# One more dt*u*B pair on POOL and one more C pair on DVE in the last batch of a Mamba and low-rank expert kernel

## The chip, the cores and the metric

The kernel runs on one core of a Trainium2 chip. The metric is the device time of one execution in microseconds, the median of several runs. All arithmetic is in float32.

## The reference, cut to what matters

Four batches of 512 rows of 512 channels pass through two residual blocks. The first one is a selective state-space scan (16 states for each of 512 channels) over a context input, and its output is gated by silu of the normalised `x`. The second is a top-2 choice of 32 low-rank experts on the normalised result. The part that the change touches is the scan:

```python
def step(state, xs):
    d_t, B_t, C_t, u_t = xs
    dA = jnp.exp(d_t[..., None] * A)
    state = state * dA + (d_t * u_t)[..., None] * B_t[:, None, :]
    y_t = jnp.einsum('ben,bn->be', state, C_t)
    return (state, y_t)
...
y = y + D[None, :, None] * u
y = y * jax.nn.silu(z)
```

The expert block then computes `sc = h @ Wr.T`, the two best of 32, `hU`, its gated product with `V`, and adds it to the residual.

## The kernel before, in words

Channels lie on the 128 partitions and time on the free axis, so that one instruction of DVE scans one state of 128 channels over a whole row of time. The work is cut into **phases** `f`. A phase is one batch, one block of 128 channels (`k` from 0 to 3) and a stretch of time: 512 steps in batches 0 to 2 (phases 0 to 11), 256 steps in the last batch, which is gone through in two halves (phases 12 to 15 with `c0` = 0, phases 16 to 19 with `c0` = 256). Where the first half ends, the last column of each state is kept in `carry`, and the second half starts from it. `SPLIT` is 12 and `LAST` is 19.

A phase has 16 **tiles** `n`, one for each state, or 8 **pairs** `p` of two. For each tile the program makes
- the decay exp(delta * A), by ACT (`decay`, L1016),
- the product dt*u*B, in one of two ways: by PE, as matmuls of the transposed `du` with diagonal matrices of B, into a PSUM bank (`make_dbu`, L759), or by POOL for a pair at a time into SBUF (`times_b`, L571). `POOL_SETS[b]` lists the pairs by POOL for each batch,
- the scan, by DVE (`scan`, L1267). For a tile by PE, the product lies in one of the three banks `p_s` and the decay in the ring `da`; for a tile by POOL it is the decay that lies in the bank. Either way a tile holds bank `g % 3`, with g = 16f + n, and the bank is free again when its scan (or its product with C out of the bank) is done (`wait_for_bank`),
- the product with C: by POOL for a pair in SBUF (`times_c`, L586), or by DVE for the pairs in `PAIRS_BY_DVE`, whose scans are written to the bank and read out of it (`times_c` of DVE, L1285),
- the sum over states: PE transposes each tile into `p_y` (`add_y`, L781).

Every engine's order is written out by hand in program order; an engine never passes a waiting instruction. Between the tiles of phase f lie the steps of the expert block of earlier tiles of rows: `best_two` (DVE, after the scan of tile 2), `gates` (DVE, after the scans of tiles 4 to 6; the last result is `gw`, L1364), `copy_gated` (ACT, L972, placed after the decay of tile 5), the product with V (PE, `times_v`, L814, at tiles 5 to 7), the product with U (PE, `times_u_weights`, L805, from tile 8 on; it waits for `gw`), and `gate_y` (DVE, L1293 and L1301, after the scans of tiles 8 and 9), for which PE's `skip` (L770) of the next phase's sum waits.

The diagonal matrices of B are written into `pair_b` at the start of a batch by POOL (`diagonals`, L544), by ACT for the last PE pair; for POOL's pairs the rows of B are broadcast into the same place by SP's queue (`broadcast_b`, L419), as those of C are into `c_bc`. `dbu` has room for two pairs: `times_b` waits for the scans of the pair before the last one (`ve_scan`). POOL also makes `du` of the next phase (`times_u`, L556) and small scales (`scale_of_f`, L605 and L607; in phases 13 and 14 these stand right after the first dbu of the next phase).

In the last batch before the change, POOL makes dbu of pairs 0, 2, 3, 5, 6, PE those of pairs 1, 4, 7. DVE multiplies pairs 1 and 4 with C (in phase 19 pair 7 as well), POOL the others. POOL takes the first two dbu of the coming phase after its C pairs 5 and 6 of the current one:

```python
times_c(f, 5)
if next_first:
    times_b(f + 1, pool_pairs(PHASE[f + 1][0])[0])
...
times_c(f, 6)
if next_first and len(pool_pairs(PHASE[f + 1][0])) == 5:
    times_b(f + 1, pool_pairs(PHASE[f + 1][0])[1])
...
times_c(f, 7)
```

Of the kernel before, what the change touches and what calls it, by code (L numbers as in the profile page):

```python
# [22 lines left out]

POOL_SETS = [[2, 5], [1, 3, 5, 7], [1, 3, 5, 7], [0, 2, 3, 5, 6]]


def flamingo(nc, x, ctx_t, g_xattn, g_ffn, in_w_t, conv_w, conv_b, x_w_t, dt_w_t, dt_b, a_log, d_skip,
# [18 lines left out]
    PHASE = [(b, k, 0, L) for b in range(B - 1) for k in range(Q)]  # L46
    PHASE += [(B - 1, k, c0, H) for c0 in (0, H) for k in range(Q)]
    F = len(PHASE)
    LAST = F - 1
    SPLIT = Q * (B - 1)  # L50
# [10 lines left out]
    def pool_pairs(b):  # L61
        return POOL_SETS[b]

    def pe_pairs(b):
        return [p for p in range(PAIRS) if p not in POOL_SETS[b]]

    def by_act(b, p):


        return p == pe_pairs(b)[-1] or b == 0 and p in (0, 6)  # L70
# [26 lines left out]

    PAIRS_BY_DVE = [(LAST, 7)]
    PAIRS_BY_DVE += [(f, p) for f in range(SPLIT, F) for p in (1, 4)]
    PAIRS_BY_DVE += [(f, 1) for f in range(Q - 1, SPLIT)] + [(f, 5) for f in range(Q - 1, SPLIT, Q)]  # L100
# [52 lines left out]
    with ExitStack() as ctx:  # L153
# [362 lines left out]
        def _(eng):  # L516
# [13 lines left out]

            def diagonals(b, i):
                p = pe_pairs(b)[i]
                if by_act(b, p):
                    return
                if i == 0 or b == 0:
# [78 lines left out]
            for f in range(F):  # L614
                b, k, c0, w = PHASE[f]
# [3 lines left out]
                many = len(pairs) >= Q  # L619
                five = len(pairs) == 5  # L620
                next_first = f < LAST and (PHASE[f + 1][0] != b or many)
                times_c(f, 0)
                if five:
                    times_b(f, pairs[2])
                elif many or len(pairs) == 3:
                    times_b(f, pairs[1])
# [5 lines left out]
                times_c(f, 1)  # L632
                if many and not five:
                    times_b(f, pairs[2])
                if turned:
                    diagonals(b, len(pe_pairs(b)) - 1)
                times_c(f, 2)
                if five or not many:
                    times_b(f, pairs[3] if five else pairs[-1])
                early_u = k == 0 and c0 == 0  # L640
# [3 lines left out]
                if many:  # L644
                    times_b(f, pairs[-1])
                if f < LAST and not (early_u and not many):
# [16 lines left out]
                times_c(f, 6)  # L663
                if next_first and len(pool_pairs(PHASE[f + 1][0])) == 5:
                    times_b(f + 1, pool_pairs(PHASE[f + 1][0])[1])
# [850 lines left out]
```

## Time and profile before

| what | value |
|---|---|
| median of three runs | 534.21 us (533.29, 534.21, 534.3) |
| the profiled execution | 533.53 us |
| its span, first to last instruction | 531.8 us |
| granted TensorE clock, mean | 0.978 |
| busy share PE, DVE, POOL, ACT | 92%, 87%, 85%, 71% |
| chain that ended last, by engine | PE 48%, POOL 19%, DVE 13%, ACT 10%, issue 9% |

The profile is of one execution. A row of a timeline gives the start and the duration of an instruction (or of several in a row, with xN) and, in brackets, how long the engine had been idle before it and what released it. Times are microseconds from the start of the span. The last batch (phases 12 to 19) takes from about 366 to 507. The chain goes back from the last instruction through whatever released each step. Instructions that follow each other on one engine overlap by up to a tenth of a microsecond, so that starts, not ends, give the pace.

### The profile page before, as it was taken

The numbers are of one execution on the slowest core, as the hardware profiler recorded it, in microseconds if no ns is written. First come the engines' busy times: TensorE is split into PE (matmuls) and PEld (weight loads), VectorE is DVE, ScalarE is ACT, GpSimd is POOL, SyncE is SP. The second block draws the span as 40 slices with busy tenths as digits, with TensorE's granted clock in tenths as the row PEclk, the third lists the DMA queues.
The fourth block names the chain that finished last, engine by engine and source line by source line (L and its number), as shares of the span: only waits on it lengthen the run. The fifth ranks groups of instructions, "written<-read, shape, count | busy, mean of one in ns | idle before, by whom it ended". The sixth has DMA issues, their size and how long they took to land.

```text
span 531.8 us, 9178 instructions
## 1 busy us (share of the span) xinstructions
PE 491.4 (92%) x3018; PEld 368.0 (69%) x3018; DVE 462.9 (87%) x846; ACT 380.1 (71%) x699; POOL 451.9 (85%) x327
## 2 busy tenths in 40 slices
PE   9989899998787999999999999999899999899688
PEld 5568788687676676668676777767566766676654
DVE  3799799799799999799999999798988989999852
ACT  4698848775876777866958776957868869768542
POOL 1389999959999999989999999889799898888910
PEclk9969799999999999999999999999999999999899
DMA  5595000126520001065230000077100000000001
GB/s 127 176 375 217 0 2 1 41 85 213 182 80 1 1 1 60 1 229 202 71 101 2 20 1 22 8 281 227 45 21 1 22 20 17 6 21 21 2 20 39
DMA packets 18704, 39.36 MB, mean 74 GB/s; under 512 B 5585, under 2 KB 6353, under 8 KB 18658
## 3 DMA queue, kind: packets, MB, share of 16 engines
q1 hardware_dynamic: 18658, 38.79, 21.4%
q8 instruction: 24, 0.39, 0.3%
q14 instruction: 22, 0.18, 0.1%
HBM read 34.33 MB, written 4.46 MB: 73 GB/s over the span
## 4 chain that ended last, share of the span: by engine, by line
PE 48%; POOL 19%; DVE 13%; ACT 10%; issue 9%; DMA 1%; DVEq 0%; SPq 0%; POOLq 0%; ACTq 0%
PE p_s L759 12%; PE p_y L781 11%; POOL state L586 9%; POOL dbu L571 7%; DVE state L1267 6%; PE p_v L814 5%; PE p_f L805 5%; PE p_tr L728 3%; PE p_v L691 2%; ACT da L1016 2%; DVE x L1216 2%; PE p_pr L703 2%; ACT pair_b L1000 1%; PE p_f L794 1%; PE p_pr L682 1%
## 5 line engine op out<-in xcount | busy, mean ns | idle before, releaser
L586 POOL TENSOR_TENSOR state<-state,c_bc 128x1024 f32<-128x1024 f32 (+1 forms) x131 | 256.7, 1970 | 21.6 <-DVE state L1267 19.2
L759 PEld LDWEIGHTS p_s<-pair_b,du_t 128*128 128x128 f32 x1072 | 140.7, 200 | 44.9 <-issue 33.4
L759 PE MATMUL p_s<-pair_b,du_t 128*128 128x128 f32 x1072 | 154.6, 287 | 16.0 <-DVE state L1267 15.8
L781 PE MATMUL p_y<-ident,state 128*128 128x128 f32 x1024 | 149.3, 276 | 0.0
L1016 ACT ACTIVATE p_s<-delta,a_neg 128x512 f32<-128x512 f32 (+1 forms) x162 | 93.7, 583 | 77.6 <-DVE state L1267 44.1
L1267 DVE TENSOR_TENSOR_SCAN state<-da,p_s 128x512 f32<-128x512 f32 (+1 forms) x116 | 134.5, 1172 | 16.0 <-PE p_s L759 13.1
L571 POOL TENSOR_TENSOR dbu<-du,pair_b 128x1024 f32<-128x1024 f32 (+1 forms) x80 | 145.3, 1819 | 0.2 <-DMA pair_b<-bc_rows 0.2
L781 PEld LDWEIGHTS p_y<-ident,state 128*128 128x128 f32 x1024 | 121.5, 144 | 23.3 <-issue 20.2
L1016 ACT ACTIVATE da<-delta,a_neg 128x512 f32<-128x512 f32 (+1 forms) x158 | 99.3, 647 | 18.5 <-DVE state L1267 18.4
L1267 DVE TENSOR_TENSOR_SCAN state<-p_s,dbu 128x512 f32<-128x512 f32 (+1 forms) x100 | 97.6, 996 | 7.6 <-POOL dbu L571 6.0
L805 PE MATMUL p_f<-u_sb,h_t 128*128 128x512 f32 x112 | 55.4, 597 | 2.4 <-DVE gw L1364 2.4
L814 PE MATMUL p_v<-v_sb,hug_t 128*128 128x512 f32 x112 | 55.4, 598 | 0.0
L1285 DVE TENSOR_TENSOR state<-p_s,c_bc 128x256 f32<-128x256 f32 (+1 forms) x58 | 30.5, 526 | 0.7
L544 POOL TENSOR_SCALAR_AFFINE_SELECT pair_b<-b_t 128x1024 f32<-128x1024 f32 x11 | 12.4, 1133 | 19.9 <-ACT b_t L972 19.9
L1267 DVE TENSOR_TENSOR_SCAN state<-p_s,carry,dbu 128x256 f32<-128x256 f32 x40 | 28.0, 734 | 0.8 <-POOL dbu L571 0.7
L805 PEld LDWEIGHTS p_f<-u_sb,h_t 128*128 128x128 f32 x112 | 18.5, 191 | 12.7 <-issue 9.6
L1267 DVE TENSOR_TENSOR_SCAN p_s<-p_s,dbu 128x512 f32<-128x512 f32 x22 | 26.8, 1217 | 0.0
L1216 DVE SCALAR_TENSOR_TENSOR u<-p_pr,cw,u 128x511 f32<-128x511 f32 (+2 forms) x33 | 24.1, 730 | 2.2 <-ACT u L936 2.1
L770 PEld LDWEIGHTS p_y<-ident,skipped 128*128 128x128 f32 x64 | 7.2, 143 | 24.5 <-issue 24.5
L814 PEld LDWEIGHTS p_v<-v_sb,hug_t 128*128 128x128 f32 x112 | 18.1, 190 | 8.4 <-issue 8.3
L556 POOL TENSOR_TENSOR du<-delta,u 128x512 f32<-128x512 f32 (+1 forms) x19 | 19.8, 1043 | 2.8 <-POOL dbu L571 2.8
L682 PE MATMUL p_pr<-cx,w_in 128*128 128x512 f32 x44 | 21.5, 612 | 0.0
(175 smaller groups left out, 640.6 us busy)
## 6 DMA issues: line engine op xcount, KB each, us to landing
c_bc<-bc_rows SPq DMA_DIRECT2D x32, 512.0 KB, 5.1
pair_b<-bc_rows SPq DMA_DIRECT2D x16, 512.0 KB, 5.5
xs<-in_x SPq DMA_DIRECT2D x16, 256.0 KB, 4.6
out<-ot SPq DMA_DIRECT2D x14, 256.0 KB, 2.0
cx<-in_ctx_t SPq DMA_DIRECT2D x4, 512.0 KB, 3.8
u_sb<-in_u_w SPq DMA_DIRECT2D x1, 1024.0 KB, 14.1
v_sb<-in_v_w SPq DMA_DIRECT2D x1, 1024.0 KB, 15.6
w_in<-in_in_w_t SPq DMA_DIRECT2D x1, 384.0 KB, 4.7
```

Source lines behind the costliest of these rows:

```text
L556: eng.tensor_tensor(du[:, 0:w], delta[:, f % 2, 0:w], u[:, (Q * b + k) % U_RING, c0:c0 + w], ALU.mult).then_inc(po_du, 1)
L571: eng.tensor_tensor(dbu[:, i % 2, :, 0:w], du[:, 0:w].unsqueeze(1).to_broadcast([P, 2, w]), rows_of_b(p)[:, :, c0:c0 + w], ALU.mult).then_ ...
L586: eng.tensor_tensor(pair, pair, c_bc[:, 2 * p:2 * p + 2, c0:c0 + w], ALU.mult).then_inc(po_cs, 1)
L682: mm = eng.matmul(conv_bank(q)[:, :], w_in[:, k, e * P:(e + 1) * P], cx[:, k, :], start=(k == 0), stop=(k == KD - 1))
L759: mm = eng.matmul(p_s[g % BANKS][:, t * P:(t + 1) * P], du_t[:, f % 2, t, :], diagonals_of(n // 2)[:, n % 2, c0 // P + t, :], start=(t == ...
L781: mm = eng.matmul(p_y[:, t, :], slot(NS * f + n)[:, t * P:(t + 1) * P], ident[:, :], is_transpose=True, start=False, stop=(n == NS - 1 and ...
L805: mm = eng.matmul(hu_bank(T)[:, :], ht_of(T)[:, k, :], u_sb[:, k, :], start=(k == 0), stop=(k == Q - 1))
L814: mm = eng.matmul(v_bank(T)[:, :], hugt_of(T)[:, k, :], v_sb[:, k, :], start=False, stop=(k == Q - 1), skip_group_check=True)
L1016: eng.activation(to, delta[:, f % 2, 0:w], ACT.Exp, scale=a_neg[:, k, n:n + 1]).then_inc(ac_da, 1)
L1216: eng.scalar_tensor_tensor(out=conv_v(q)[:, s:], in0=conv_bank(q)[:, 0:L - s], scalar=cw[:, q % Q, TAPS - 1 - s:TAPS - s], in1=conv_v(q)[: ...
L1267: eng.tensor_tensor_scan(scanned, decayed, added, first, ALU.mult, ALU.add).then_inc(ve_scan, 1)
L1285: eng.tensor_tensor(slot(g)[:, 0:w], scanned, c_bc[:, n, c0:c0 + w], ALU.mult).then_inc(ve_cs, 1)
```

## The change

In the last batch pair 1 goes from PE to POOL (dbu), and pair 7 from POOL to DVE (C) in all eight phases; the order of POOL's steps is rewritten for six pairs. Diagonals of pair 1 are no longer made, and the rows of B of pair 1 are broadcast in their place. A pair that DVE multiplies with C and POOL gives dbu for now exists in the last batch: both the decay and the scan's result of pair 1 lie in the bank.

```diff
-POOL_SETS = [[2, 5], [1, 3, 5, 7], [1, 3, 5, 7], [0, 2, 3, 5, 6]]
+POOL_SETS = [[2, 5], [1, 3, 5, 7], [1, 3, 5, 7], [0, 1, 2, 3, 5, 6]]
...
-    PAIRS_BY_DVE = [(LAST, 7)]
-    PAIRS_BY_DVE += [(f, p) for f in range(SPLIT, F) for p in (1, 4)]
+    PAIRS_BY_DVE = [(f, p) for f in range(SPLIT, F) for p in (1, 4, 7)]
...
             def diagonals(b, i):
+                if i >= len(pe_pairs(b)) or by_act(b, pe_pairs(b)[i]):
+                    return
                 p = pe_pairs(b)[i]
-                if by_act(b, p):
-                    return
...
-                five = len(pairs) == 5
+                six = len(pairs) == 6
...
                 times_c(f, 0)
-                if five:
+                if six:
                     times_b(f, pairs[2])
...
                 times_c(f, 1)
-                if many and not five:
-                    times_b(f, pairs[2])
+                if many:
+                    times_b(f, pairs[3 if six else 2])
...
                 times_c(f, 2)
-                if five or not many:
-                    times_b(f, pairs[3] if five else pairs[-1])
+                if not many:
+                    times_b(f, pairs[-1])
...
                 times_c(f, 3)
                 if many:
-                    times_b(f, pairs[-1])
+                    times_b(f, pairs[4 if six else -1])
+                if six:
+                    times_b(f, pairs[5])
...
                 times_c(f, 6)
-                if next_first and len(pool_pairs(PHASE[f + 1][0])) == 5:
+                if next_first and len(pool_pairs(PHASE[f + 1][0])) == 6:
                     times_b(f + 1, pool_pairs(PHASE[f + 1][0])[1])
```

POOL's order where phase 14 goes over into phase 15. `dbu` is a pair's dt*u*B, `state<-state,c_bc` a pair's product with C, `carry` the kept column, `fr` the small scale. Before, the first row is dbu of pair 0 of phase 15:

```order
L571 TENSOR_TENSOR dbu<-du,pair_b 128x2x256
L605 TENSOR_TENSOR fr<-fmv,minus_half 128x1
L607 TENSOR_SCALAR fr<-fmv,fr 128x1
L584 COPY carry<-state 128x2
L586 TENSOR_TENSOR state<-state,c_bc 128x2x256
L571 TENSOR_TENSOR dbu<-du,pair_b 128x2x256
L584 COPY carry<-state 128x2
L586 TENSOR_TENSOR state<-state,c_bc 128x2x256
L584 COPY carry<-state 128x2
L586 TENSOR_TENSOR state<-state,c_bc 128x2x256
L571 TENSOR_TENSOR dbu<-du,pair_b 128x2x256
```

The same place in the changed kernel, again from dbu of pair 0 of phase 15 on (its line numbers are one lower on POOL):

```order
L570 TENSOR_TENSOR dbu<-du,pair_b 128x2x256
L604 TENSOR_TENSOR fr<-fmv,minus_half 128x1
L606 TENSOR_SCALAR fr<-fmv,fr 128x1
L583 COPY carry<-state 128x2
L585 TENSOR_TENSOR state<-state,c_bc 128x2x256
L570 TENSOR_TENSOR dbu<-du,pair_b 128x2x256
L583 COPY carry<-state 128x2
L585 TENSOR_TENSOR state<-state,c_bc 128x2x256
L570 TENSOR_TENSOR dbu<-du,pair_b 128x2x256 x2
```

The second dbu stands at the same place in both, but it was that of pair 2 and is now that of pair 1; the product with C of pair 7 has left the queue, and two dbu (pairs 2 and 3) now follow each other.

DVE's order from the end of phase 17 into phase 18, before; the rows after `hug` are tiles 14 and 15 (pair 7), tiles 0 and 1, and tile 2 (the first of pair 1):

```order
L1373 TENSOR_TENSOR hug<-p_f,gw 128x512
L1267 SCALAR_TENSOR_TENSOR state<-da,carry,p_s 128x256 x2
L1267 SCALAR_TENSOR_TENSOR state<-p_s,carry,dbu 128x256 x2
L1267 SCALAR_TENSOR_TENSOR p_s<-da,carry,p_s 128x256
L1323 MAX top<-p_f 128x8
```

And in the changed kernel (line numbers one higher on DVE):

```order
L1374 TENSOR_TENSOR hug<-p_f,gw 128x512
L1268 SCALAR_TENSOR_TENSOR p_s<-da,carry,p_s 128x256
L1286 TENSOR_TENSOR state<-p_s,c_bc 128x256
L1268 SCALAR_TENSOR_TENSOR p_s<-da,carry,p_s 128x256
L1286 TENSOR_TENSOR state<-p_s,c_bc 128x256
L1268 SCALAR_TENSOR_TENSOR state<-p_s,carry,dbu 128x256 x2
L1268 SCALAR_TENSOR_TENSOR p_s<-p_s,carry,dbu 128x256
L1324 MAX top<-p_f 128x8
```

Two products with C have come in between the scans of pair 7, and the scan of tile 2 takes POOL's `dbu` in the place of PE's bank.

## Rows read from the trace of the kernel before

**Rows 1.** Stages: phase 15 (columns: us, busy per engine, PEclk, DMA share, GB/s)

```profile
416.26:434.22 17.96, 17.12 (x99) 11.75 (x98) 15.82 (x47) 12.09 (x30) 16.09 (x20) 1.00 0.08 29
```

**Rows 2.** Chain that ended last, phases 14 and 15 (start us, us, what)

```profile
418.10 0.19 POOL carry L584
...
427.41 1.24 POOL dbu L571
...
432.10 0.46 PE p_s L759 x4
```

**Rows 3.** Timeline of POOL: second dbu for phases 13, 15 and 16

```profile
386.88 1.27 POOL L571 TENSOR_TENSOR dbu<-du,pair_b 128x512 f32<-128x512 f32 x1
...
423.19 1.27 POOL L571 TENSOR_TENSOR dbu<-du,pair_b 128x512 f32<-128x512 f32 x1
...
439.44 1.27 POOL L571 TENSOR_TENSOR dbu<-du,pair_b 128x512 f32<-128x512 f32 x1
```

**Rows 4.** Timeline of DVE: scan of tile 2, phases 13, 15, 16, 17, 18

```profile
386.68 0.67 DVE L1267 TENSOR_TENSOR_SCAN p_s<-da,p_s 128x256 f32<-128x256 f32 x1
...
422.10 0.67 DVE L1267 TENSOR_TENSOR_SCAN p_s<-da,p_s 128x256 f32<-128x256 f32 x1
...
439.61 0.75 DVE L1267 TENSOR_TENSOR_SCAN p_s<-da,carry,p_s 128x256 f32<-128x256 f32 x1
...
458.51 0.73 DVE L1267 TENSOR_TENSOR_SCAN p_s<-da,carry,p_s 128x256 f32<-128x256 f32 x1
...
475.41 0.73 DVE L1267 TENSOR_TENSOR_SCAN p_s<-da,carry,p_s 128x256 f32<-128x256 f32 x1
```

**Rows 5.** Timeline of DVE: phase 15, then phase 17

```profile
423.13 0.20 DVE L1323 MAX8 top<-p_f 128x8 f32<-128x32 f32 x1 [0.36 <-PE p_f L794]
...
428.68 0.69 DVE L1267 TENSOR_TENSOR_SCAN state<-p_s,dbu 128x256 f32<-128x256 f32 x1 [0.97 <-POOL dbu L571]
...
432.59 0.69 DVE L1267 TENSOR_TENSOR_SCAN p_s<-da,p_s 128x256 f32<-128x256 f32 x1 [0.30 <-PE p_s L759]
...
460.22 0.74 DVE L1267 TENSOR_TENSOR_SCAN p_s<-da,carry,p_s 128x256 f32<-128x256 f32 x1
...
461.34 0.74 DVE L1267 TENSOR_TENSOR_SCAN state<-p_s,carry,dbu 128x256 f32<-128x256 f32 x1
...
468.30 0.76 DVE L1267 TENSOR_TENSOR_SCAN p_s<-da,carry,p_s 128x256 f32<-128x256 f32 x1 [0.63 <-PE p_s L759]
...
469.62 2.67 DVE L1267 TENSOR_TENSOR_SCAN state<-p_s,carry,dbu 128x256 f32<-128x256 f32 x4
```

**Rows 6.** Timeline of ACT: phase 15

```profile
424.58 0.58 ACT L972 ACTIVATE hug_t<-p_tr 128x512 f32<-128x512 f32 x1
```

**Rows 7.** Timeline of PE: phase 15, then phase 17

```profile
425.32 1.94 PE L814 MATMUL p_v<-v_sb,hug_t 128*128 128x512 f32 x4
...
429.26 0.61 PE L759 MATMUL p_s<-pair_b,du_t 128*128 128x128 f32 x4
...
465.93 1.88 PE L805 MATMUL p_f<-u_sb,h_t 128*128 128x512 f32 x4
```

**Rows 8.** Timeline of POOL: from phase 11 into phase 12

```profile
363.58 1.09 POOL L544 TENSOR_SCALAR_AFFINE_SELECT pair_b<-b_t 128x1024 f32<-128x1024 f32 x1
...
366.96 1.27 POOL L571 TENSOR_TENSOR dbu<-du,pair_b 128x512 f32<-128x512 f32 x1
368.18 2.37 POOL L586 TENSOR_TENSOR state<-state,c_bc 128x1024 f32<-128x1024 f32 x1
```

**Rows 9.** Timeline of DVE: phase 12, tile 4

```profile
370.05 0.68 DVE L1267 TENSOR_TENSOR_SCAN state<-p_s,dbu 128x256 f32<-128x256 f32 x1
```

**Rows 10.** DMA issues (KB each, median us to landing)

```profile
pair_b<-bc_rows SPq DMA_DIRECT2D x16, 512.0 KB, 5.5
```

**Rows 11.** Stages: two stretches of phase 19, columns as in rows 1

```profile
496.00:500.00 4.00, 1.39 (x8) 1.04 (x8) 3.29 (x7) 2.03 (x5) 4.00 (x4) 0.98 0.01 2
500.00:504.00 4.00, 3.49 (x20) 3.52 (x21) 3.28 (x7) 1.79 (x4) 3.49 (x4) 0.60 0.02 4
```

## The prediction

> **What bounds the kernel now.** I read the stages first. In phase 15 [rows 1], of 17.96 us PE is busy for 17.12 (first figure), DVE for 15.82 (third), POOL for 16.09 (fifth): three engines near their limit, so that a phase's length is set by how they wait for each other, and no share of busy time gives a price. Next the chain that ended last [rows 2]. In phases 14 and 15 it leaves DVE at 418.10, at the end of the scan of tile 11, runs through POOL without a gap, C pair 5, dbu 0, the small scale, C 6, dbu 2, C 7, C 0, dbu 3, and comes back to DVE at the scan of tile 6, which had waited 0.97 us for that last dbu at 428.68 [rows 5]. So **POOL's run after tile 11** is part of the cycle. In it I look for the end of the second dbu [rows 3] beside the start of DVE's tile 2 [rows 4]. Last come the waits of DVE further on in a phase: at tile 2's `MAX8` for PE's scores (0.36), at tile 9 for PE (0.30 in phase 15, 0.63 in phase 17) [rows 5].
>
> **The change part by part.** A tile by PE costs PE 0.46 us [rows 2] (the row of 432.10). Sixteen tiles (pair 1, eight phases) are removed: 7.4 us of PE's work. On POOL a dbu comes and a C pair goes, both 1.27 us [rows 3, 8]; in phase 19, where DVE had pair 7 before, only the dbu comes, but POOL's order up to its third dbu there loses nothing and gains nothing before tile 6. DVE gets the product with C of pair 7. What such a product costs it behind a scan shows in phase 17: from the scan of tile 3 at 460.22 to the next at 461.34 is 1.12 us, against 2.67 / 4 = 0.67 for scans without one [rows 5]. That is 0.45 a tile, 0.9 a pair (I take 1.05 where the last column is kept too, an estimate from the same rows and one more small instruction).
>
> *The new wait.* Tile 2 took its product from PE, early. Now it takes POOL's second dbu, which stands where pair 2's stood, behind C 5, dbu 0, the scale and C 6. Pair 2 was wanted only at tile 4; pair 1 is wanted at tile 2. The second dbu ended at 386.88 + 1.27 = 388.15, 424.46 and 440.71 in phases 13, 15 and 16 [rows 3], and DVE began tile 2 at 386.68, 422.10 and 439.61 [rows 4]: it will be **late by 1.47, 2.36 and 1.10 us**. Phase 14 repeats phase 15. POOL's run up to there starts from tile 11's scan as before and holds nothing that has gone, so none of it gets shorter. DVE's own delay by pair 7 (1.05) lies inside this wait. In phases 17 and 18 POOL has no columns to keep and phase 18 no scale; there the dbu comes with or before DVE, and what counts is DVE's own 0.9.
>
> *What is given back.* Behind tile 2 the wait for scores (0.36) goes, since PE is early; so does the 0.97 at tile 6, since dbu 3 now follows dbu 2 at once and C 7 is out of the queue. But the steps behind tile 2 form a second path: its product with C frees the bank for ACT's decay of tile 5, behind it ACT copies `hug_t` (start 424.58 [rows 6]), PE starts the product with V on it at 425.32, reaches its tile 8 at 429.26 [rows 7], needs 0.46 for that, and from the product with U to tile 9's scan go 468.30 - 465.93 = 2.37 us [rows 5, 7]. From tile 2 to tile 9 that is (424.58 - 422.10 - 0.36) + 0.74 + 3.94 + 0.46 + 2.37 = 9.6 us. Before, it was 432.59 - 422.10 = 10.5. **Given back: 0.9** in phases 14 and 15. In phase 17 it was 468.30 - 458.51 = 9.8, of which the same path leaves 9.5: 0.3, and I use that for 16 and 18. Phase 13 lies between these two; I take 0.5. PE's freed 0.46 a tile lies ahead of the product with V and turns into a wait there: it is worth nothing in this sum.
>
> *Phases 12 and 19.* POOL loses one writing of diagonals (1.09) and gets to the second dbu at 366.96 - 1.09 = 365.87. Behind it come C 7 of phase 11 (2.37) and C 0, and only then dbu 2 [rows 8]: 367.1 + 2.3 + 1.5 + 1.25 = 372.2 (1.5 is C 0 of 256 columns with its kept column, an estimate from 1.27 and the 0.19 of [rows 2]), where DVE wanted tile 4 at 370.05 [rows 9]. Most of this 2.1 falls into waits that are there now for PE and ACT; I take +0.3, between -0.5 (PE's relief counts) and +1.5. In phase 19 nothing of the expert block follows and POOL's third dbu decides as before; +0.2, between -0.5 and +0.9, from pair 7 of phase 18.
>
> *Moved transfers.* SP's queue gets one broadcast more, 512 KB, 5.5 us from issue to landing [rows 10], for pair 1, and its slot goes ahead of that of pair 2. Pair 1 was POOL's in batch 2, so its place is free early in phase 11, long before use. The broadcasts of C behind it wait for POOL's own reading of the old rows, not for the queue. Cost nothing; without that cover a landing would come later by up to one broadcast, 5.5 us. In pair 1 ACT's decay now goes into the bank and so waits for the scan or the product three tiles before; DVE stands waiting at tile 2 in that time, which hides it; otherwise it costs up to one decay, about 0.5. A scan with both operands in other memory (`dbu` and bank in place of `da` and bank) has no such row at 256 columns. The nearest scans are 0.67 to 0.69 for either kind [rows 4, 5]; bounds -0.05 and +0.1 a tile, 0 taken.
>
> *Sum.* 12: +0.3. 13: 1.47 - 0.5 = +1.0. 14 and 15: 2.36 - 0.86 = +1.5 each. 16: 1.10 - 0.3 = +0.8. 17 and 18: 0.92 - 0.3 = +0.6 each. 19: +0.2. Together **+6.4 us**. The profiled execution took 533.53, so the same one would take 539.9; the median of the runs is 0.7 above it, and my forecast for the median is 540.6. Ends of this case, from the bounds above: +3 (give-backs of 1.4 a phase) to +8.
>
> **TensorE's clock.** The row first: in phase 19 PE is busy for 1.39 of 4 us, and in the next 4 the granted clock is 0.60, that is 1.2 GHz for most of them [rows 11]; that cost (1 - 0.60) x 4 = 1.6 us of its time. In the changed phases 13 to 15 PE stands idle for about 3 of 5 us ahead of the product with V: 1.3 of removed work, plus the 2.4 by which tile 2 is late, less what PE was behind. The Trainium skill ("TensorE: Matmul & The Clock Gate", on HAM oscillation) warns of just this, that waits between bursts throttle the array and each burst then starts at half clock; by it the sum would rise in all three phases. The sum above has no such fall; it is a rival.
>
> **The rivals.**
> - *The clock falls in one to three phases.* For: the row of phase 19. Against: the pause here is shorter and broken by a microsecond and a half of matmuls. PE's path is then the critical one, so each fall counts in full: 540.6 + 1.6 = 542.2, or 545.4 for three.
> - *PE set the pace, and it gets faster.* For: 95% busy in rows 1, and DVE waits for PE at tile 9. If the second dbu were there when DVE comes to tile 2, at most 1.05 us later than now, the phases would be shorter by PE's 0.92 each: 534.2 - 7.4 = 526.8. It decides whether POOL's run from tile 11 to the second dbu (424.46 - 418.10 = 6.4 us) is shorter than DVE's way there (4.0 + 1.05). It is not, by 1.3 us; POOL would have to run ahead, which its wait on tile 11 forbids. Where the two are level, in 17 and 18, half of the gain is possible.
> - *No change.* The lateness of tile 2 is caught up whole before tile 9, because the copy of `hug_t` can go sooner than I think, and pair 7 is hidden: 534.2 to 537.
> - *The change does not do what it says*: the order rows show that it does; no chance.
>
> **How the numbers follow.** The forecast case (537.2 to 542) has a chance of 0.58; the clock 0.24; faster 0.09; little change 0.09. About 0.2%, 1.1 us, can be told from no change by a measurement of this kernel. Faster by more than that: 0.09. Within it, half of the fourth case: 0.05. Slower: 0.86. The range takes in the forecast case whole, the upper half of the last one and two and a half falls of the clock: 535.0 to 545.0.
>
> **What would show each step.** In the changed profile: DVE's scan of tile 2 waits for POOL's dbu, about 1.3 us in phases 14 and 15, less in 13 and 16, near zero in 17 and 18; no wait for POOL at tile 6 in 13 to 18; PE idle ahead of the product with V in 13 to 15; DVE's products of pair 7 add 14 instructions; phase 15 takes 19.4 us instead of 17.96. POOL's busy time stays within 2 us. I am wrong if tile 2 does not wait, if tile 9 follows tile 2 by less than 9 us, or if PE's clock falls outside phase 19.

## The result and the profile after

| | before | changed |
|---|---|---|
| median | 534.25 us (4 runs, 533.29 to 535.01) | 551.84 us (4 runs, 549.47 to 554.63) |
| profiled execution, its span | 533.53, 531.8 us | 549.47, 547.7 us |
| granted TensorE clock, mean | 0.978 | 0.963 |

The ratio is 1.0335, 95% interval 1.0306 to 1.0364: 17.6 us slower. The direction was forecast; the size was not. 540.6 was expected, and the range ended at 545.0. The runs of the changed kernel also lie 5.2 us apart, three times as far as those of before.

The page of the changed kernel (busy tenths and granted clock in 40 slices of 13.7 us):

```profile
PE 492.4 (90%) x2954; PEld 362.8 (66%) x2954; DVE 469.9 (86%) x868; ACT 381.0 (70%) x699; POOL 451.9 (83%) x323
...
PE   8969898989687999999989999999779899899588
...
PEclk9979899999899999999999999999999799699799
...
PE 46%; POOL 18%; DVE 14%; ACT 12%; issue 9%; DMA 1%; DVEq 0%; SPq 0%; ACTq 0%; POOLq 0%
```

Busy shares fall by one or two points and the chain has nearly the shares of before. What stands out is the line `PEclk`. Before, it reads 9 from the slice of 67 us up to the last batch's end, where a single 8 stands. Now the last batch (366 to 523 us) has a 7 in the slice of 424 us, a 6 in that of 465 and a 7 in that of 506. So I cut the last batch at the same event in both traces, the start of DVE's scan of tile 11, and looked at the stretches that end in phases 14, 15 and 17. Before (columns as in [rows 1]):

```profile
399.38:417.34 17.96, 17.12 (x98) 11.76 (x97) 15.81 (x47) 15.65 (x34) 16.23 (x21) 1.00 0.05 16
417.34:434.52 17.18, 16.34 (x93) 11.21 (x92) 15.07 (x46) 11.37 (x28) 15.67 (x20) 1.00 0.04 16
452.35:470.29 17.94, 16.04 (x93) 11.04 (x92) 16.70 (x45) 11.49 (x28) 15.87 (x16) 1.00 0.04 16
```

The same three in the changed kernel, and below them the pieces of each in which the granted clock is at half:

```profile
400.42:421.39 20.97, 17.82 (x90) 11.26 (x89) 16.96 (x51) 15.72 (x34) 16.01 (x19) 0.92 0.04 13
421.39:443.02 21.63, 18.57 (x85) 11.37 (x84) 16.21 (x50) 11.61 (x28) 16.02 (x19) 0.84 0.04 13
461.57:484.82 23.25, 19.80 (x85) 13.00 (x84) 17.52 (x47) 11.80 (x28) 15.97 (x16) 0.78 0.03 12
410.17:413.60 3.43, 3.28 (x4) 1.41 (x5) 3.15 (x14) 3.28 (x12) 2.61 (x4) 0.51 0.00 0
430.50:437.50 7.00, 6.20 (x11) 2.91 (x12) 5.10 (x19) 4.38 (x13) 5.10 (x7) 0.51 0.00 0
468.10:478.40 10.30, 9.97 (x29) 6.58 (x30) 7.68 (x25) 6.82 (x18) 6.98 (x8) 0.50 0.00 1
```

PE executes eight records fewer in each stretch and is busy longer, 18.57 us against 16.34 in phase 15, because for 7.0 us it runs at 1.2 GHz in place of 2.4 (a granted clock of 0.51). POOL's work is unchanged within 0.4 us. Over the span, the stretches of phases 14, 15 and 17 grow by 3.01, 4.45 and 5.31 us, 12.8 of the 15.9 by which the span grows.

What PE did before it fell is in its timeline (changed kernel, phases 14, 15 and 16, then 17):

```profile
410.32 3.55 PE L815 MATMUL p_v<-v_sb,hug_t 128*128 128x512 f32 x4 [1.67 <-ACT hug_t L973]
...
426.25 0.41 PE L729 MATMUL p_tr<-ident,zh 128*128 128x128 f32 x2 [0.98 <-ACT h_t L973]
...
431.31 3.75 PE L815 MATMUL p_v<-v_sb,hug_t 128*128 128x512 f32 x4 [1.68 <-ACT hug_t L973]
...
451.96 1.95 PE L815 MATMUL p_v<-v_sb,hug_t 128*128 128x512 f32 x4 [0.54 <-ACT hug_t L973]
...
468.43 0.66 PE L729 MATMUL p_tr<-ident,zh 128*128 128x128 f32 x2 [2.52 <-ACT h_t L973]
```

In 14 and 15 PE waits twice, about 1.0 us for ACT's copy of `h_t` and 1.7 us for that of `hug_t`; the clock falls in the second wait, and the product with V, 1.94 us in [rows 7], takes 3.55 and 3.75. In 16 the wait is 0.54 us, the clock holds and the product takes 1.95. In 17 the wait of 2.52 us comes earlier, and the clock stays at half through 9.97 us of busy matmuls out of 10.3. What that does to DVE is seen in its timeline (changed kernel: tile 2 and tile 9 of phase 15, then `MAX8` and tile 9 of phase 17):

```profile
428.54 0.70 DVE L1268 TENSOR_TENSOR_SCAN p_s<-p_s,dbu 128x256 f32<-128x256 f32 x1 [1.22 <-ACT p_s L1017]
...
438.92 0.70 DVE L1268 TENSOR_TENSOR_SCAN p_s<-da,p_s 128x256 f32<-128x256 f32 x1 [2.97 <-PE p_s L760]
...
470.67 0.20 DVE L1324 MAX8 top<-p_f 128x8 f32<-128x32 f32 x1 [1.47 <-PE p_f L795]
...
480.67 0.76 DVE L1268 TENSOR_TENSOR_SCAN p_s<-da,carry,p_s 128x256 f32<-128x256 f32 x1 [3.05 <-PE p_s L760]
```

Tile 2 waits as forecast. Tile 9, which waited 0.30 and 0.63 us for PE in [rows 5], now waits 3 us.

### The profile page after: what moved, and what is told of

It reads as the page before. It is cut to its first block, busy times and chain, and to the rows that moved or that the text cites. A ratio compares the mean times of both kernels' runs of the same rounds, so it can differ in the third digit from the quotient of the medians.

```text
span 547.7 us, 9076 instructions
## 1 busy us (share of the span) xinstructions
PE 492.4 (90%) x2954; PEld 362.8 (66%) x2954; DVE 469.9 (86%) x868; ACT 381.0 (70%) x699; POOL 451.9 (83%) x323
## 4 chain that ended last, share of the span: by engine, by line
PE 46%; POOL 18%; DVE 14%; ACT 12%; issue 9%; DMA 1%; DVEq 0%; SPq 0%; ACTq 0%; POOLq 0%
PE p_s L760 10%; PE p_y L782 10%; POOL state L585 8%; PE p_v L815 7%; POOL dbu L570 6%; DVE state L1268 6%; PE p_f L806 5%; PE p_tr L729 3%; ACT da L1017 2%; PE p_v L692 2%; ACT p_s L1017 2%; DVE x L1217 2%; ACT pair_b L1001 2%; DVE p_s L1268 1%; PE p_pr L704 1%
## 5 line engine op out<-in xcount | busy, mean ns | idle before, releaser
L585 POOL TENSOR_TENSOR state<-state,c_bc 128x1024 f32<-128x1024 f32 (+1 forms) x124 | 247.8, 2009 | 28.5 <-DVE state L1268 26.5
L1017 ACT ACTIVATE p_s<-delta,a_neg 128x256 f32<-128x256 f32 (+1 forms) x178 | 101.2, 573 | 89.8 <-DVE state L1286 45.2
L760 PEld LDWEIGHTS p_s<-pair_b,du_t 128*128 128x128 f32 x1008 | 130.0, 197 | 41.1 <-issue 31.1
L570 POOL TENSOR_TENSOR dbu<-du,pair_b 128x512 f32<-128x512 f32 (+1 forms) x88 | 154.5, 1766 | 0.6 <-DMA pair_b<-bc_rows 0.3
L760 PE MATMUL p_s<-pair_b,du_t 128*128 128x128 f32 x1008 | 141.2, 283 | 13.6 <-DVE state L1268 13.3
L1268 DVE TENSOR_TENSOR_SCAN state<-da,p_s 128x512 f32<-128x512 f32 x108 | 129.3, 1209 | 14.7 <-PE p_s L760 11.9
L1017 ACT ACTIVATE da<-delta,a_neg 128x512 f32<-128x512 f32 (+1 forms) x142 | 91.8, 663 | 18.3 <-DVE state L1268 18.3
L815 PE MATMUL p_v<-v_sb,hug_t 128*128 128x512 f32 x112 | 62.0, 661 | 4.7 <-ACT hug_t L973 4.5
L1286 DVE TENSOR_TENSOR state<-p_s,c_bc 128x256 f32<-128x256 f32 (+1 forms) x72 | 36.4, 506 | 0.9
L1268 DVE TENSOR_TENSOR_SCAN p_s<-p_s,dbu 128x512 f32<-128x512 f32 (+1 forms) x30 | 32.3, 1077 | 3.5 <-ACT p_s L1017 2.4
L815 PEld LDWEIGHTS p_v<-v_sb,hug_t 128*128 128x128 f32 x112 | 20.2, 211 | 15.9 <-issue 15.8
L806 PEld LDWEIGHTS p_f<-u_sb,h_t 128*128 128x128 f32 x112 | 18.5, 191 | 12.8 <-issue 9.6
```

The lines of the kernel that those rows point to most:

```text
L570: eng.tensor_tensor(dbu[:, i % 2, :, 0:w], du[:, 0:w].unsqueeze(1).to_broadcast([P, 2, w]), rows_of_b(p)[:, :, c0:c0 + w], ALU.mult).then_ ...
L585: eng.tensor_tensor(pair, pair, c_bc[:, 2 * p:2 * p + 2, c0:c0 + w], ALU.mult).then_inc(po_cs, 1)
L760: mm = eng.matmul(p_s[g % BANKS][:, t * P:(t + 1) * P], du_t[:, f % 2, t, :], diagonals_of(n // 2)[:, n % 2, c0 // P + t, :], start=(t == ...
L806: mm = eng.matmul(hu_bank(T)[:, :], ht_of(T)[:, k, :], u_sb[:, k, :], start=(k == 0), stop=(k == Q - 1))
L815: mm = eng.matmul(v_bank(T)[:, :], hugt_of(T)[:, k, :], v_sb[:, k, :], start=False, stop=(k == Q - 1), skip_group_check=True)
L1017: eng.activation(to, delta[:, f % 2, 0:w], ACT.Exp, scale=a_neg[:, k, n:n + 1]).then_inc(ac_da, 1)
```

## The experiments

Times are compared with runs of the kernel before on the same chip. Two questions stood open: how much of the 17.6 us is the clock's, and what the rest is made of. A matmul of the identity with itself into the block of `p_y` that is unused in these phases (`fill`) keeps PE busy and delays nothing as long as it lies in a wait.

**1. The changed kernel with PE's waits filled** (`fill`). The table's first number stands ahead of `turn_sz` at tile 2, the second ahead of `times_v` at tile 5. By the table these are 46 matmuls, 92 records in the trace (the expectation says 42).

```diff
+            def fill(count):
+                for i in range(count):
+                    eng.matmul(p_y[:, 3, :], ident[:, :], ident[:, :], start=False, stop=False,
+                               skip_group_check=True)
+
+            FILL = {13: (9, 1), 14: (4, 6), 15: (4, 6), 16: (1, 2), 17: (9, 1), 18: (1, 2)}
...
+                        fill(FILL.get(f, (0, 0))[0])
                         if f:
                             turn_sz(f - 1)
...
                     if n == 5 and tail >= 0:
+                        fill(FILL.get(f, (0, 0))[1])
```

> The changed kernel, with matmuls of the identity into an unused block of p_y where PE waits in phases 13 to 18 (ahead of the turn of silu(z) and of the product with V; 3 to 10 a phase, 42 in all, about 9 us of PE). Theory A: the clock stays at 2.4 GHz in phases 13 to 18, and the 6 windows of half clock there, 1.6 us each, go: 541 to 544 us, the late dbu stays. If the clock is not what stretches phases 14, 15 and 17: 551 us or more, since PE only got more work.

Measured: 541.81 us (541.49 to 542.04), ratio 1.0145 [1.0122, 1.0167]. The same three stretches of this kernel:

```profile
400.89:419.47 18.58, 17.67 (x105) 12.44 (x104) 16.14 (x49) 14.91 (x32) 15.42 (x19) 1.00 0.01 2
419.47:438.83 19.36, 18.56 (x110) 13.00 (x109) 16.91 (x51) 12.26 (x30) 16.01 (x20) 1.00 0.07 28
457.00:476.00 19.00, 17.56 (x103) 12.24 (x102) 17.48 (x47) 11.69 (x29) 15.31 (x16) 1.00 0.06 22
```

(The first is 0.8 us short of a whole stretch, and the second begins with that piece; phase 14 takes 19.39 us from tile 11 to tile 11 and phase 15 takes 18.58.) More work on PE, and the kernel is 10.0 us faster: with more to do PE keeps a granted clock of 1.00. In phase 15 its timeline reads

```profile
423.99 1.06 PE L835 MATMUL p_y<-ident 128*128 128x128 f32 x8
...
428.36 1.50 PE L835 MATMUL p_y<-ident 128*128 128x128 f32 x12
430.17 1.96 PE L815 MATMUL p_v<-v_sb,hug_t 128*128 128x512 f32 x4 [0.31 <-ACT hug_t L981]
```

The product with V starts 1.65 us behind the matmul that stands ahead of the fillers, as in the changed kernel (1.68), but it takes 1.96 us. The runs lie 0.55 us apart, where those of the changed kernel lie 5.2 apart. So the spread goes with the falls: over the changed kernel's four runs the mean clock goes from 0.963 in the fastest to 0.951 in the slowest.

**2. The removed matmuls put back as idle ones** (`same_pe`): four identity matmuls in each of phases 13 to 18, where tiles 2 and 3 were made.

```diff
+            FILL = {f: (4, 0) for f in range(13, 19)}
```

> The changed kernel, with four matmuls of the identity in phases 13 to 18 at the place of the removed tiles 2 and 3, so that PE has the same work as before and the engines' other work is as changed. If the removed work itself opens the way to the half clock, the falls go and it takes 541 to 544 us. If it is the waiting time behind it (the product with V waits for the copy of hug_t, 1.7 us in phases 14 and 15), it stays at 547 to 552 us.

Measured: 547.24 us (ratio 1.0259 [1.0232, 1.0286]), but the five runs are 541.96 and then 546.93, 547.24, 547.28 and 547.86. The run of 541.96 is the profiled one, and it has no fall in phases 13 to 18:

```profile
400.80:419.50 18.70, 16.43 (x92) 10.92 (x91) 16.21 (x50) 14.96 (x33) 15.52 (x19) 1.00 0.00 1
419.50:438.90 19.40, 17.23 (x96) 11.62 (x97) 16.91 (x51) 12.62 (x31) 16.07 (x20) 1.00 0.08 28
457.00:476.00 19.00, 16.63 (x95) 11.20 (x92) 17.48 (x46) 12.15 (x29) 15.19 (x17) 1.00 0.08 29
```

Of the other four only the mean clock is on record, 0.956 to 0.963 against 0.972. So the same program takes 542 us where the clock holds and 547 us where it is lower; with the removed work put back as four fillers a phase it can come out either way.

**3. `h_t` copied one tile sooner** (`h_first`). A tuning idea against the waits for `h_t`.

```diff
-                    if n == (1 if mid % Q else 2) and mid >= 0:
+                    if n == ((1 if mid % Q else 2) if f < SPLIT else (0 if mid % Q else 1)) and mid >= 0:
                         copy_h(mid)
```

> The changed kernel, with ACT's copy of h_t one tile sooner in the last batch (ahead of the decay of tile 1, in phases 13 and 17 ahead of the decay of tile 2), so that it no longer stands behind a decay that waits for DVE's product of pair 7. Theory D (the decays in the bank hold up h_t, PE waits 2.6 us for it in phases 13 and 17 and 1.0 in 14 and 15, and this idle time brings the clock down): 543 to 548 us, no fall in phases 13 and 17. Theory A alone (only the dbu at tile 2 matters): 549 to 553 us.

Measured: 550.13 us (548.07 to 551.81), 1.0312 [1.0271, 1.0354]. From the waits of phases 12 to 19, first of the changed kernel, then of this one (us in total, times, longest):

```profile
PE p_tr L729 <- ACT h_t L973: 7.9, 6, 2.6
```

```profile
PE p_tr L729 <- ACT h_t L973: 3.6, 6, 1.5
PE p_tr L729 <- ACT sz_t L973: 5.1, 6, 2.3
```

The wait halved, 2.3 us of the 4.3 came back as one for the next copy, `sz_t` (2.8 us in 3 waits in the changed kernel), and the clock still falls, from 386.4 to 393.2, 410.3 to 417.2, 434.2 to 437.7 and 468.4 to 478.6. Idle time that moves is still idle.

**4. One half of the change alone.** C of pair 7 to DVE in all phases, nothing else (`c7_alone`, against before):

```diff
-    PAIRS_BY_DVE = [(LAST, 7)]
-    PAIRS_BY_DVE += [(f, p) for f in range(SPLIT, F) for p in (1, 4)]
+    PAIRS_BY_DVE = [(f, p) for f in range(SPLIT, F) for p in (1, 4, 7)]
```

> The kernel before, with the product of pair 7 with C on DVE in all eight phases of the last batch and nothing else changed. Theory A (the late second dbu of POOL makes tile 2 wait, PE then idles and its clock falls): pair 1 still comes from PE, so tile 2 does not wait and the clock falls in phase 19 alone; DVE has 14 products more, of which POOL's shorter run to the third dbu gives back about 1 us in phases 14 and 15. 534 to 539 us. Theory B (the products of pair 7 on DVE are what costs): 545 us or more, as the changed kernel.

Measured: 543.15 us (539.65 to 544.39), 1.0157 [1.011, 1.0204]. And dbu of pair 1 to POOL alone, the reverse edit on the changed kernel (`dbu1_alone`):

```diff
-    PAIRS_BY_DVE = [(f, p) for f in range(SPLIT, F) for p in (1, 4, 7)]
+    PAIRS_BY_DVE = [(LAST, 7)]
+    PAIRS_BY_DVE += [(f, p) for f in range(SPLIT, F) for p in (1, 4)]
```

> The changed kernel, with the product of pair 7 with C back on POOL (phase 19 excepted, as before). Theory A: the second dbu ends at the same distance from tile 11, DVE gets to tile 2 about 1 us sooner and waits that much longer, and POOL's queue is a product longer up to the third dbu: 548 to 556 us, with the clock at 1.2 GHz in several phases. Theory B: under 538 us.

Measured: 551.35 us (549.27 to 554.42), 1.031 [1.0276, 1.0345]. Both halves bring falls of the clock in phases 13 to 18: `c7_alone` one of 10.2 us in phase 13, `dbu1_alone` four, in 13, 14, 15 and 17. The first shows a way that I had not seen at all. Its PE timeline in phase 13, and the stretch behind:

```profile
386.33 0.93 PE L758 MATMUL p_s<-pair_b,du_t 128*128 128x128 f32 x4 [1.73 <-DVE state L1284]
```

```profile
386.70:396.90 10.20, 10.20 (x35) 7.51 (x35) 7.44 (x28) 5.93 (x16) 6.91 (x9) 0.50 0.01 2
```

Tile 2's matmuls need the bank of tile 15 of the phase before, which DVE's product of pair 7 now holds. PE waits 1.73 us for it, and then it is busy for 10.20 of 10.20 us at half clock.

**5. Both halves with the clock held** (`c7_fill`: `c7_alone` with 28 identity matmuls ahead of tile 2; `dbu1_fill`: `dbu1_alone` with the table of experiment 1).

```diff
+            FILL = {13: 7, 14: 5, 15: 5, 16: 2, 17: 7, 18: 2}
...
+                    if n == 2:
+                        fill(FILL.get(f, 0))
                     if (f, n) in by_pe:
                         make_dbu(f, n)
```

> The kernel c7_alone with 28 matmuls of the identity in phases 13 to 18, ahead of PE's tile 2, where PE waits 1.2 to 1.7 us a phase for DVE's product of tile 15 to free the bank. c7_alone took 543.2 and had three windows at half clock in its profile. With the clock held, about 1.6 us a window go: 538 to 540 us, which is the price of the product of pair 7 beside a PE tile 2. If the filler comes on top of PE's path: 543 us or more.

> The kernel fill with the product of pair 7 with C back on POOL. Theory A: in phases 13 to 16 DVE's work for pair 7 lies in the wait at tile 2 and costs nothing, while C 7 in POOL's queue puts off dbu 2 and 3 by 1.5 us: 542 to 545 us. Rival E: the products of pair 7 are what costs: 536 to 539 us.

Measured: `c7_fill` 539.97 us (538.73 to 540.4), 1.0105 [1.0084, 1.0126]; `dbu1_fill` 546.12 us (545.02 to 546.35), 1.0227 [1.0208, 1.0245]. Neither has a fall in phases 13 to 18. By the ratios, and in this kernel's 534: pair 7 on DVE costs 5.6 us, dbu of pair 1 on POOL costs 12.1, both together 7.7 (experiment 1). With pair 7 on POOL the third dbu, tile 4's, has one more C product ahead of it; DVE in phase 15 of `dbu1_fill`, tiles 2 and 4:

```profile
427.57 0.70 DVE L1277 TENSOR_TENSOR_SCAN p_s<-p_s,dbu 128x256 f32<-128x256 f32 x1 [2.30 <-POOL dbu L571]
...
431.75 0.69 DVE L1277 TENSOR_TENSOR_SCAN state<-p_s,dbu 128x256 f32<-128x256 f32 x1 [1.52 <-POOL dbu L571]
```

So moving pair 7 is right given the first move (it gives 4.4 us back), and wrong without it. In all three kernels the clock falls later on, from about 505 us, for 6.8, 10.2 and 6.8 us, and these prices hold what that costs. From tile 11 of phase 11 to tile 11 of phase 19 alone, the three are 4.9, 11.4 and 7.8 us longer than before, in the same order.

**6. Is tile 2's wait the whole of what remains?** First both dbu of the coming phase ahead of C 5 (`early_dbu`), then the same with the fillers of experiment 1 (`early_fill`):

```diff
+                front = next_first and f >= SPLIT
+                if front:
+                    times_b(f + 1, pool_pairs(PHASE[f + 1][0])[0])
+                    times_b(f + 1, pool_pairs(PHASE[f + 1][0])[1])
                 times_c(f, 5)
-                if next_first:
+                if next_first and not front:
...
-                if next_first and len(pool_pairs(PHASE[f + 1][0])) == 6:
+                if next_first and not front and len(pool_pairs(PHASE[f + 1][0])) == 6:
```

> The changed kernel, with both dbu of the coming phase ahead of the product of pair 5 with C on POOL, in phases 12 to 18. Same work on every engine. Theory A: tile 2 finds its dbu some 3.5 us earlier and does not wait; now dbu 2 is late at tile 4 by about 1 us, behind C 5, C 6 and C 0, while PE's path to the product with V is free: 536 to 541 us, clock falls in none or one of phases 13 to 18. Theory B: no change, 550 us.

> The changed kernel with both earlier edits: the two dbu of the coming phase ahead of C 5, and the 42 matmuls of the identity in PE's waits. Theory A (lateness of the second dbu is most of what the full clock leaves): fill alone gave 541.8; if the order of POOL gives tile 2 its product in time, 537 to 540 us. Rival C: in that order C 5 and C 6 come late for PE's sum of the phase before and dbu 2 late for tile 4, so POOL's run as a whole is what counts and nothing is won: 541 to 544 us, with PE waiting for POOL's C in p_y.

Measured: 547.76 us (546.34 to 551.04), 1.0264 [1.0216, 1.0311], and 547.34 us (546.77 to 548.04), 1.0256 [1.0229, 1.0282]. The second is slower than `fill` by 5.5 us, nearly all of it in phases 13 (22.51 us against 19.67) and 17 (21.45 against 18.92). C 5 and C 6 now come late, and PE's sum of tiles 10 to 13 waits for them, with everything behind it (waits of phases 12 to 19, `early_fill`):

```profile
DVE top L1336 <- PE p_f L799: 8.0, 4, 3.6
...
PE p_y L786 <- POOL state L585: 7.1, 7, 1.8
...
POOL dbu L570 <- DVE p_s L1280: 3.7, 2, 1.9
POOL dbu L570 <- DVE state L1280: 3.7, 5, 1.5
```

In `fill` the first is 0.5 us and the others are absent. It is also not free of falls: two of 3.4 us, from 388.4 and 466.9, since the fillers lie where `fill` had its waits. `early_dbu` has two falls of 10.2 us in the same two phases. As whole runs these two give no clean answer. The next is `borrow_fill`: `fill`, but tiles 2 and 3 take the dbu of pair 0, which is there early, and POOL makes the second dbu in its place in the order and nobody reads it. It leaves pair 1's own B out of the result. Since tiles 2 and 3 now read pair 0's room, POOL's third dbu, which goes into it, must also wait for the scan of tile 3.

```diff
+                    if before >= SPLIT and q == 0:
+                        q = 1
+                    if before >= SPLIT and i % 6 != by_pool[SPLIT, 0] % 6:
+                        eng.wait_ge(po_dbu, i - 1)
                     eng.wait_ge(ve_scan, NS * before + 2 * q + 2)
...
                 elif on_pool(f, n):
-                    i = by_pool[f, n // 2]
+                    i = by_pool[f, 0 if f >= SPLIT and n // 2 == 1 else n // 2]
```

> The kernel fill, in which DVE's scans of tiles 2 and 3 in the last batch take pair 0's dbu instead of pair 1's (this leaves out the use of pair 1's B; POOL still makes the dbu of pair 1, nobody reads it). Tile 2 then doesn't wait for the second dbu. Theory A (the late second dbu is the larger part of the 7.6 us that are left with the clock held): 536 to 539 us. Rival E (the 14 products of pair 7 on DVE, and the queue of POOL as a whole, are the larger part): 540 to 542 us.

Measured: 542.81 us (542.08 to 544.1), 1.0171 [1.015, 1.0192]; as a whole not faster than `fill`. DVE in phase 15, tiles 2 and 4:

```profile
425.66 0.67 DVE L1280 TENSOR_TENSOR_SCAN p_s<-p_s,dbu 128x256 f32<-128x256 f32 x1
...
429.66 0.69 DVE L1280 TENSOR_TENSOR_SCAN state<-p_s,dbu 128x256 f32<-128x256 f32 x1 [1.36 <-POOL dbu L574]
```

Tile 2 comes without a wait, 5.84 us behind tile 11 where `fill` has 7.13. Tile 4 follows 4.00 us later instead of 2.71, and 5.84 + 4.00 = 9.84 is what `fill` takes to tile 4 as well (7.13 + 2.71 = 9.84). The third dbu stops it. Yet phases 14 and 15 take 18.82 and 18.01 us from tile 11 to tile 11, 0.57 less than in `fill`. What is lost again lies in phases 13 and 16 to 19, which take 0.1 to 0.7 us longer, 2.0 together, and there the test's own wait counts: POOL stands idle for 0.6 to 1.5 us ahead of the third dbu, until the scan of tile 3 is done, while in 14 and 15 it goes straight on. Its row in phase 17:

```profile
466.48 1.27 POOL L574 TENSOR_TENSOR dbu<-du,pair_b 128x512 f32<-128x512 f32 x1 [1.48 <-DVE p_s L1280]
```

`early_dbu` has no such wait, and between its two falls its clock holds. Its phases 14 and 15 from tile 11 to tile 11, and below them those of `c7_alone`, in which pair 1 is still PE's:

```profile
404.68:423.27 18.59, 16.63 (x90) 10.74 (x89) 16.66 (x52) 15.32 (x33) 15.71 (x19) 1.00 0.01 4
423.27:441.07 17.80, 15.90 (x85) 10.17 (x84) 15.89 (x50) 12.02 (x29) 15.39 (x19) 1.00 0.08 28
404.82:423.35 18.53, 16.87 (x98) 11.69 (x97) 16.82 (x52) 15.59 (x34) 14.78 (x18) 1.00 0.04 15
423.35:441.07 17.72, 16.05 (x93) 11.11 (x92) 16.05 (x50) 11.35 (x28) 14.77 (x18) 1.00 0.05 17
```

So at full clock pair 7 on DVE costs 0.57 and 0.54 us in these two phases (17.96 and 17.18 before). Pair 1's dbu on POOL, with tile 2 in time, adds 0.06 and 0.08, although tile 4 then waits 1.4 us for POOL. The lateness of tile 2 adds the other 0.80 and 0.78 (19.39 and 18.58 in `fill`). `early_dbu` also lacks the fillers, but they don't explain this: `same_pe`, with four a phase instead of ten, takes 19.40 and 18.59. For the other phases no run at full clock separates the terms.

**7. Shorten POOL's run instead.** If POOL's run from tile 11 sets the pace, then the two small scale instructions in it (`fr`, L604 and L606) are worth moving: 0.56 + 0.26 us. In the last batch's first half they are put off into the next phase, ahead of C 4 (`after_fr_fill`, on `fill`):

```diff
+                if f > SPLIT + 1 and STATS.get(f - 1) and PHASE[f - 1][1]:
+                    scale_of_f(STATS[f - 1][0])
                 times_c(f, 4)
...
-                if k and STATS.get(f):
+                if k and STATS.get(f) and f < SPLIT:
                     scale_of_f(STATS[f][0])
```

> The kernel fill with POOL's small scale of phases 13 and 14 put off as in before_fr, so that POOL's run from tile 11 to the second and third dbu is 0.87 us shorter in phases 14 and 15 and nothing else changes. If POOL's run as a whole sets tiles 2 and 4 (rival C, which early_fill and borrow_fill point to): 540.0 to 540.8 us, with tile 11 to tile 2 at 6.3 in phases 14 and 15 instead of 7.1. If another path (PE's product with V, DVE's own work) is level with it: 541.8 us as fill.

Measured: 541.06 us (539.77 to 541.84), 1.0135 [1.0115, 1.0155]. The intervals of this and of `fill` overlap, but the trace is clear: tile 11 to tile 2 is 6.27 and 6.29 us in phases 14 and 15 against 7.14 and 7.13, and the whole stretches are 0.57 and 0.55 shorter. Phase 16 takes 0.40 more (18.94 against 18.54).

**8. The same on the kernel before** (`before_fr`), which has 13 fillers (into the idle bank `p_pr`) around tile 9 of phase 19 besides; these alone are `before_fill19`.

```diff
+                    if f == LAST and n == 9:
+                        fill_last(4)
                     if (f, n) in by_pe:
                         make_dbu(f, n)
+                    if f == LAST and n == 9:
+                        fill_last(9)
```

> The kernel before, with 13 matmuls of the identity into the idle bank p_pr in phase 19, where PE waits ahead of tile 9 and of the skip matmuls. If a window at half clock costs about 1.6 us of PE on the path there, that window goes and the kernel takes 532.5 to 533.5 us; if DVE's own chain sets phase 19, 534.

> The kernel before with the matmuls in phase 19 (532.97 us), and POOL's small scale (0.87 us of POOL's run from tile 11 to the third dbu) put off from phases 13 and 14 into the next phase, ahead of C 4. By the chain of the kernel before, DVE waits 0.97 us for the third dbu at tile 6 of phases 14 and 15: up to 1.7 us go, 531.3 to 532.5 us. If PE sets the length of these phases as well: 533.

Measured: `before_fill19` 532.97 us (10 runs, 532.12 to 534.19), 0.9985 [0.9971, 0.9999]; `before_fr` 531.46 us (6 runs, 530.63 to 531.94), 0.9952 [0.9938, 0.9967]. Phase 19 of `before_fill19`, the stretches of [rows 11]:

```profile
496.00:500.00 4.00, 3.53 (x31) 3.56 (x32) 3.27 (x7) 2.13 (x6) 4.00 (x4) 1.00 0.01 2
500.00:504.00 4.00, 3.72 (x34) 3.44 (x32) 4.00 (x8) 2.03 (x5) 3.51 (x4) 1.00 0.01 4
```

The clock of 0.60 is gone; by the ratio it was worth 0.8 us (0.05 to 1.5). The deferral gives 1.8 more (0.9985 against 0.9952 of 534): the wait of tile 6 for the third dbu, 0.97 us in [rows 5], is down to 0.1 in `before_fr` (phase 15, tiles 4, 5 and 6):

```profile
423.63 0.68 DVE L1277 TENSOR_TENSOR_SCAN state<-p_s,dbu 128x256 f32<-128x256 f32 x1
...
424.94 0.68 DVE L1277 TENSOR_TENSOR_SCAN state<-p_s,dbu 128x256 f32<-128x256 f32 x1
...
426.33 0.69 DVE L1277 TENSOR_TENSOR_SCAN state<-p_s,dbu 128x256 f32<-128x256 f32 x1
```

Phases 14 and 15 take 17.45 and 16.64 us from tile 11 to tile 11 instead of 17.96 and 17.18. Those are 1.05 us of the 1.8. The rest isn't in the last batch, whose other phases are as long as in `before_fill19`. Between the two profiled executions 1.3 us more lie ahead of phase 12, where the edit changes nothing and the mean clock is 0.98 in one and 0.97 in the other, so that part of the 1.8 may be chance. This kernel beats both.

## Why the prediction was wrong, step by step

With the clock held, experiment 1 measured what the sum had tried to say. From tile 11 to tile 11, in us:

| phase | 13 | 14 | 15 | 16 | 17 | 18 | 19 |
|---|---|---|---|---|---|---|---|
| before | 18.36 | 17.96 | 17.18 | 17.83 | 17.94 | 16.95 | 14.04 |
| changed | 19.68 | 20.97 | 21.63 | 18.55 | 23.25 | 17.49 | 14.91 |
| changed, filled | 19.67 | 19.39 | 18.58 | 18.54 | 18.92 | 17.49 | 14.91 |
| filled less before | 1.31 | 1.43 | 1.40 | 0.71 | 0.98 | 0.54 | 0.87 |
| forecast | 1.0 | 1.5 | 1.5 | 0.8 | 0.6 | 0.6 | 0.2 |
| changed less filled | 0.01 | 1.58 | 3.05 | 0.01 | 4.33 | 0.00 | 0.00 |
| clock at half in it | 0 | 3.4 | 7.0 | 0 | 10.3 | 0 | 4.7 (filled 3.1) |

**The sum was nearly right.** Forecast +6.4 us with phase 12 (its terms add up to 6.5); measured 7.2, and 7.8 with the 0.55 of phase 12, for which it had 0.3. The lateness of tile 2 in phases 14 and 15 was to be 2.36 us: tile 11 to tile 2 went from 4.75 and 4.76 to 7.14 and 7.13, which is 2.39 and 2.37. The way from tile 2 to tile 9 was to be 9.6 us, and 9.5 in phase 17's kind: in the filled kernel it is 9.52 and 9.52, and 9.45 and 9.43 in 16 and 18; in 17 itself it is 10.03, of which more below. The wait at tile 6 is gone. Experiment 6 bears out that this wait and this way are what costs in 14 and 15: 0.8 us of the 1.4 are tile 2's lateness, most of the rest is pair 7. 541.8 us was measured against a forecast of 540.6.

**The step that failed is the price and the chance of the clock.** The prediction put one fall at 1.6 us, in one to three phases, with "545.4 for three" as the worst and 0.24 as its chance. Falls came in 14, 15 and 17, and they lasted 3.4, 7.0 and 10.3 us. In phases 13 to 18 the last two rows of the table match phase for phase: 20.7 us at half clock (in stretches where the granted clock reads 0.50 or 0.51) cost 9.0, or 0.43 us for each. Had every one of those counted in full it would be 0.5. One fall is thus 1.6 only where it is as short as that of [rows 11]; the first was, at 1.58, and the other two cost two and nearly three times as much. The argument against it, "the pause here is shorter and broken by a microsecond and a half of matmuls", was drawn from a single row of before and did not hold: the clock fell in a wait of 1.7 us that came 5 us behind one of 1.0. A fall outside phase 19 was one of the prediction's own signs of being wrong.

The pause itself had been read nearly rightly ("about 3 of 5 us ahead of the product with V": 0.98 + 1.68 = 2.7 were measured in phase 15, out of 6.0). The Trainium skill ("TensorE: Matmul & The Clock Gate", "A second HAM failure mode: psum-queue depth-cycling") describes a kernel whose PE idles briefly between groups of matmuls and loses throughput to re-throttling. The trace agrees with it, and by that rule the fall should have been the main case.

**Phase 17 was missed for a second reason.** I had costed ACT's decay of pair 1 into the bank at nothing, hidden in DVE's wait at tile 2, and PE's idle time was expected in 13 to 15 alone. DVE's wait does hide it from DVE. It does not from PE. Pair 7 by DVE holds the banks of tiles 14 and 15 longer, and ACT's decays of tiles 1 and 2 stand ahead of its copy of `h_t` (ACT, changed kernel, phase 17):

```profile
464.18 0.80 ACT L1059 ACTIVATE h<-x,fr 128x512 f32<-128x512 f32 x1
...
466.17 0.48 ACT L1017 ACTIVATE p_s<-delta,a_neg 128x256 f32<-128x256 f32 x1 [1.19 <-DVE state L1286]
467.29 0.48 ACT L1017 ACTIVATE p_s<-delta,a_neg 128x256 f32<-128x256 f32 x1 [0.64 <-DVE state L1286]
467.71 0.58 ACT L973 ACTIVATE h_t<-p_tr 128x512 f32<-128x512 f32 x1
```

The copy starts 467.71 - 464.18 = 3.5 us behind the step before it in the expert block, `h` (2.2 us before the change, with one decay in the bank ahead of it), and PE waits 2.52 us for it. I had asked who waits for DVE and not who stands behind the waiting decay on ACT. With the clock held this costs 0.98 - 0.6 = 0.4 us in phase 17, and 4.3 more through the clock. In phase 13 the same wait is 2.60 us, and there, in this execution, no fall followed; in `h_first` and `dbu1_alone` one did. Why it falls in one execution and not in another stays open.

**Smaller misses.** In phase 19 +0.2 was forecast and +0.87 measured. PE is at half clock for 6.8 us in all there and right behind it (changed and filled) where before had 3.4, but up to tile 11 that isn't the cause: changed and filled take the same 14.91, `before_fill19` without the fall of [rows 11] takes 14.04 as before, and `same_pe`, with 8 us at half clock in this stretch, only 15.02. The loss lies ahead of tile 2, which comes 6.28 us behind tile 11 in place of 5.14, the products of pair 7 of phase 18. Phase 13 cost 0.3 more than forecast. The bracket at tile 2 in 14 and 15 names ACT's decay, but what came in time with the scan was POOL's dbu (427.24 + 1.27 = 428.51, the scan at 428.54). By the order of ACT's rows tile 2's own decay had ended almost 2 us earlier; the one that ends at 428.53 is for tile 4. In `borrow_fill`, where the dbu is early, tile 2 does not wait at all.

**The rivals.** The faster one, PE as the pace, is refuted, though not by `fill`, whose fillers give PE its work back. In phases 14 and 15 of `early_dbu` tile 2 finds its dbu, the clock holds and PE is busy for less (16.63 us in 14 against 17.12), and the phases are longer than before all the same (18.59 and 17.80 against 17.96 and 17.18). "No change" is refuted by `fill` too. The rival that came true was the clock's, with 17.6 - 7.7 = 9.9 us where the most it allowed was 3 x 1.6 = 4.8.

## What to carry to other kernels

Work taken off an engine that has a clock to keep isn't free: where the change makes that engine wait, price the fall of the clock by how long it may last, not by the shortest one in the trace, and take the pause as a warning in each repetition of the loop. A few idle matmuls in a wait tell in one run how much of a slowdown is the clock's. And where a test takes one wait away and brings another, or a fall of the clock, compare it stage by stage: as whole runs, `early_fill` and `borrow_fill` are no faster than `fill`, while in the two phases where nothing else came in between, `borrow_fill` gains 0.6 us each and `early_dbu` 0.8.

## What the runs showed that I had not expected

- At half clock PE can be busy without a gap and not get its clock back for long: 10.20 of 10.20 us in `c7_alone`, 9.97 of 10.30 in phase 17 of the changed kernel. In the last batch of these traces a fall lasted between 3.4 and 10.3 us.
- One program can come out at either of two times: 541.96 us, or 546.9 to 547.9, for `same_pe` on one chip, and the changed kernel spread over 5.2 us where its filled form spread over 0.55.
- Adding 46 matmuls of no use made a kernel 10.0 us faster; adding 13 made the kernel before 0.8 us faster.
